# Graph network kernel: rebuilt eigenvector stage and changed Householder step

## The reference

```
deg = sum(A, axis=0) + sum(A, axis=1) - diagonal(A)
L_norm = d_inv_sqrt[:, None] * (diag(deg) - A) * d_inv_sqrt[None, :]
_, U = eigh(L_norm)
agg = einsum('mn,bnd->bmd', U.T, features)
h = relu(agg @ W1 + b1);  out = h @ W2 + b2
return einsum('nm,bmd->bnd', U, out)
```

## Time and profile before

| | us |
|---|---|
| median of 3 runs (lowest to highest) | 1511.3 (1510.47 to 1511.42) |
| profiled execution, its own time | 1511.8 |
| its span, first to last instruction | 1510.0 |

### The profile page before, as it was taken

The page is one execution under the profiler, slowest core; times in us unless marked ns, Lnnn a source line. Parts: engine busy times, 40 slices in busy tenths (PEclk is TensorE's granted clock), DMA queues, the critical chain, the costliest instruction groups (busy, mean ns, idle before and its releaser), DMA issues.

```text
span 1510.0 us, 22169 instructions
## 1 busy us (share of the span) xinstructions
PE 1105.1 (73%) x5407; PEld 673.1 (45%) x5407; DVE 1023.0 (68%) x4055; ACT 743.4 (49%) x2047; POOL 306.4 (20%) x1038
## 2 busy tenths in 40 slices
PE   3777777777542340158788568999999999479997
PEld 2444555555421130145453356444454444346665
DVE  7777887777779999855676744444434353757876
ACT  2444444444342436024466457775545554367775
POOL 4045555555346551000000000000011030000000
PEclk9999999999999995569998689999999999589999
DMA  5000000000110000000000000000000000000001
GB/s 143 1 1 1 1 1 1 1 2 1 22 31 1 1 0 1 1 0 0 0 0 0 0 0 0 0 0 0 1 0 0 0 1 0 0 8 21 28 21 36
DMA packets 16657, 12.33 MB, mean 8 GB/s; under 512 B 665, under 2 KB 14530, under 8 KB 16578
## 3 DMA queue, kind: packets, MB, share of 16 engines
q1 hardware_dynamic: 16578, 11.49, 2.7%
HBM read 7.23 MB, written 4.19 MB: 8 GB/s over the span
## 4 chain that ended last, share of the span: by engine, by line
PE 53%; DVE 32%; issue 6%; ACT 6%; DMA 1%; DVEq 1%; ACTq 0%; POOL 0%; POOLq 0%
PE P L1370 31%; PE P L704 10%; DVE scal L337 2%; ACT arena L656 2%; DVE arena L467 2%; PE P L1512 2%; DVE arena L521 2%; DVE arena L523 2%; DVE bst_all L922 1%; DVE arena L472 1%; DVE bcol L366 1%; ACT hb L1177 1%; DVE arena L465 1%; PE P L1505 1%; DVE arena L343 1%
## 5 line engine op out<-in xcount | busy, mean ns | idle before, releaser
L1370 PE MATMUL P<-arena,WT 128*128 (+2 forms) x792 | 329.0, 579 | 3.9 <-ACT L1263 2.9
L1370 PEld LDWEIGHTS P<-arena,WT 128*128 128x128 f32 x792 | 151.9, 192 | 181.0 <-issue 167.1
L704 PE MATMUL P<-arena 1*128 1x127 f32 (+62 forms) x504 | 163.0, 431 | 80.8 <-ACT arena L656 57.4
L1276 ACT ACTIVATE arena<-P,bl 128x512 f32<-128x512 f32 (+1 forms) x252 | 153.5, 636 | 139.0 <-PE P L1370 131.6
L704 PEld LDWEIGHTS P<-arena 1*128 1x128 f32 x504 | 124.1, 306 | 132.7 <-DVE arena L347 109.3
L911 POOL COPY arena<-arena 128x512 f32<-128x512 f32 x16 | 21.2, 1366 | 647.0 <-DVE arena L1101 555.2
L1090 DVE TENSOR_TENSOR arena<-arena 128x512 f32<-128x512 f32 (+1 forms) x36 | 22.0, 610 | 137.5 <-ACT arena L1276 137.5
L648 ACT ACTIVATE arena<-arena 1x127 f32<-1x127 f32 (+62 forms) x126 | 32.2, 256 | 154.9 <-DVE arena L358 144.6
L1177 ACT ACTIVATE hb<-xN,nmr,rsd 128x128 f32 (+1 forms) x192 | 78.6, 482 | 55.8 <-PE P L1370 46.9
L197 POOL TENSOR_SCALAR lf<-lf 1x1 f32<-1x1 f32 x210 | 86.1, 410 | 21.9
L704 PE MATMUL P<-arena,Ib 128*128 128x46 bf16 (+1 forms) x318 | 35.5, 273 | 64.0 <-ACT arena L678 63.4
(11 more groups left out here) (497 smaller groups left out, 2514.3 us busy)
## 6 DMA issues: line engine op xcount, KB each, us to landing
out_dram<-xN SPq DMA_DIRECT2D x16, 256.0 KB, 2.3
Wn<-in_L_gnn_Wih_dram SPq DMA_DIRECT2D x4, 256.0 KB, 2.9
Wn<-in_L_gnn_Whh_dram SPq DMA_DIRECT2D x4, 256.0 KB, 2.9
Wqkv<-in_L_gnn_W_dram SPq DMA_DIRECT2D x1, 192.0 KB, 3.6
W1n<-in_L_gnn_W_dram SPq DMA_DIRECT2D x1, 128.0 KB, 4.1
W2n<-in_L_gnn_W_dram SPq DMA_DIRECT2D x1, 128.0 KB, 3.9
Wg<-in_L_gnn_Wg_dram SPq DMA_DIRECT2D x2, 64.0 KB, 3.6
adj<-in_adj_dram SPq DMA_DIRECT2D x1, 64.0 KB, 1.8
```

The costliest lines, as they stand in the source:

```text
L704: def mm(o,l,r,start=True,stop=True): return t.matmul(o,lhsT=l,rhs=r,start=start,stop=stop)
L1276: act(s.gt[u][gate][:,0:cols],P[4*u+gate][:,0:cols],f,bias=s.bl[:,4*(p-1)+gate:4*(p-1)+gate+1]).then_inc(ev('lstm_gates'),1)
L1370: def mm(o,l,r,start=True,stop=True,**k): return t.matmul(o,lhsT=l,rhs=r,start=start,stop=stop,**k)
```

## The change

In the reflector loop:
- The floor operation on the norm goes; a constant of 1e-30 is given to the square root as its bias instead (a pointer). h is formed from the root alone.
- x becomes a column by a transpose instead of a product, and b becomes a row by a product over the columns k to 127 instead of a transpose over all 128.
- v is scaled as soon as the reciprocal is there: ScalarE does the elements from k+2 on, and VectorE the two in front, after the addition to x0 and behind Bv. The wait for the addition moves from p to this multiply.
- The first spot of leaf work moves from ahead of Bv to behind it.

In the eigenvector stage: three squares go to ScalarE and two products and the handling of the gaps go to GpSimd; the leaf sign is sent round in the recurrence; the seven signs come from one maximum, one comparison and one dot product in place of a chain; the eigenvalues of the first estimate are kept for both rounds of correction, so that gaps and their reciprocals are formed once, and Rayleigh quotients and the second and third row broadcast go; XnXn is multiplied earlier; input_variance, bias_columns and input_scale are put at other places.

Beside that, semaphores are merged (masks and iota; all parameters' loads; weights_T; residual_x and the like), with wait values to match. The diff, cut:

```diff
+        e=Chain(eng,ev('gpsimd_step'))
+        e.n=c.n
+        eng.wait_ge(ev('twisted'),1)
+        e.mark(tt(inv_up[:,1:N],inv_up[:,1:N],off[:,1:N],ALU.mult))
+        tt(inv_down[:,0:N-1],inv_down[:,0:N-1],off[:,1:N],ALU.mult).then_inc(ev('eigen_from_gpsimd'),1)
+        eng.wait_ge(ev('gaps'),1)
+        e(tt(far[:,:],gap[:,:],gap[:,:],ALU.mult))
+        e(ts(far[:,:],far[:,:],4e-12,None,ALU.is_ge))
+        e.mark(ts(half_near[:,:],far[:,:],0.5,-0.5,ALU.mult,ALU.add))
+        e(ts(near[:,:],far[:,:],-1.0,1.0,ALU.mult,ALU.add))
+        tt(gap[:,:],gap[:,:],near[:,:],ALU.add).then_inc(ev('eigen_from_gpsimd'),1)
         net.gpsimd_windows(eng)
...
-            c.mark(stt(scal[:,3:4],x0,-1.0,x0,ALU.mult,ALU.min))
-        sign_of_x0(0)
+            return c.mark(stt(scal[:,3:4],x0,-1.0,x0,ALU.mult,ALU.min))
+        signed=[sign_of_x0(0)]
         def hh_step(k):
             u,x_next=reflector(k),reflector(k+1)
             x0=u[:,k+1:k+2]
-            v.wait_ge(ev('column_norm2'),k+1)
-            floor=c.mark(ts(scal[:,4:5],scal[:,7:8],-1.0,-1e-30,ALU.mult,ALU.min))
-            c.wait(floor)
+            c.wait(signed[k])
             v.wait_ge(ev('column_norm'),k+1)
-            h=c.mark(ts(scal[:,2:3],scal[:,9:10],scal[:,3:4],scal[:,4:5],ALU.mult,ALU.add))
+            h=c.mark(stt(scal[:,2:3],scal[:,3:4],scal[:,9:10],scal[:,9:10],ALU.subtract,ALU.mult))
             sr=c.mark(ts(scal[:,1:2],scal[:,0:1],-1.0,scal[:,9:10],ALU.add,ALU.mult))
             c.wait(h)
-            ih=c.mark(v.reciprocal(scal[:,10:11],scal[:,2:3]))
-            c.wait(ih)
+            v.reciprocal(scal[:,10:11],scal[:,2:3]).then_inc(ev('v_scale'),1)
+            c.wait(sr)
             v.wait_ge(ev('column_psum'),k+1)
             tt(x0,x0,scal[:,1:2],ALU.add).then_inc(ev('v_unscaled'),1)
-            if k>=LEAF_FROM: leaf_at(2*(k-LEAF_FROM))
             v.wait_ge(ev('row_b'),k+1)
             v.wait_ge(ev('row_xB'),k+1)
             stt(Bv_row[:,k:N],b_row[:,k:N],scal[:,1:2],P[1][0:1,k:N],ALU.mult,ALU.add).then_inc(ev('Bv'),1)
+            v.wait_ge(ev('v_scale'),k+1)
             v.wait_ge(ev('v_unscaled'),k+1)
+            ts(v_row[:,k:k+2],u[:,k:k+2],scal[:,10:11],None,ALU.mult).then_inc(ev('v_scaled'),1)
+            if k>=LEAF_FROM: leaf_at(2*(k-LEAF_FROM))
             v.wait_ge(ev('Bv'),k+1)
             vp=c.mark(ttr(unused_row[:,k+1:N],u[:,k+1:N],Bv_row[:,k+1:N],scal[:,5:6]))
-            v.wait_ge(ev('v_scaled'),k+1)
+            v.wait_ge(ev('v_scaled'),2*k+2)
             x1=c.mark(stt(x1_row[:,k+2:N],Bv_row[:,k+2:N],v_row[:,k+1:k+2],b_row[:,k+2:N],ALU.mult,ALU.add))
...
+            if i==LEAF_SIGN:
+                v.wait_ge(ev('leaf_from_gpsimd'),5*SWEEPS-1)
+                tt(leaf[:,14:15],leaf[:,0:1],leaf[:,0:1],ALU.mult).then_inc(ev('leaf_sign'),1)
...
+        v.sem_inc(ev('twisted'),1)
         c(tt(G[:,:],G[:,:],D_down[:,:],ALU.subtract))
         c(tt(G[:,:],D_up[:,:],G[:,:],ALU.subtract))
-        c(tt(Y_work[:,:],D_down[:,:],D_down[:,:],ALU.mult))
-        c(tt(Y[:,:],D_up[:,:],D_up[:,:],ALU.mult))
+        c(tt(A_X[:,:],G[:,:],G[:,:],ALU.mult))
+        v.wait_ge(ev('squared'),2)
         c(tt(Y_work[:,:],Y_work[:,:],Y[:,:],ALU.add))
-        c(tt(Y[:,:],G[:,:],G[:,:],ALU.mult))
-        c(stt(Y_work[:,:],Y_work[:,:],(8*EPS)**2,Y[:,:],ALU.mult,ALU.add))
+        c(stt(Y_work[:,:],Y_work[:,:],(8*EPS)**2,A_X[:,:],ALU.mult,ALU.add))
...
-        c(ttr(Y_work[:,:],choice[:,:],G[:,:],col[:,6:7]))
-        c(ts(Y_work[:,:],choice[:,:],1.0,None,ALU.subtract))
-        c(tt(inv_up[:,1:N],inv_up[:,1:N],off[:,1:N],ALU.mult))
-        c(tt(inv_up[:,1:N],inv_up[:,1:N],Y_work[:,1:N],ALU.mult))
-        c(v.memset(inv_up[:,0:1],0.0))
-        c(tt(inv_down[:,0:N-1],inv_down[:,0:N-1],off[:,1:N],ALU.mult))
-        c(tt(inv_down[:,0:N-1],inv_down[:,0:N-1],Y_work[:,0:N-1],ALU.mult))
-        c(v.memset(inv_down[:,N-1:N],0.0))
-        c(v.tensor_tensor_scan(Y[:,:],inv_up[:,:],choice[:,:],0.0,ALU.mult,ALU.add))
+        c.mark(ttr(Y_work[:,:],choice[:,:],G[:,:],col[:,6:7]))
+        v.wait_ge(ev('eigen_from_gpsimd'),1)
+        up=c.mark(stt(inv_up[:,1:N],choice[:,1:N],-1.0,inv_up[:,1:N],ALU.add,ALU.mult))
+        down=c.mark(stt(inv_down[:,0:N-1],choice[:,0:N-1],-1.0,inv_down[:,0:N-1],ALU.add,ALU.mult))
+        c.wait(up)
+        c.mark(v.tensor_tensor_scan(Y[:,:],inv_up[:,:],choice[:,:],0.0,ALU.mult,ALU.add))
+        c.wait(down)
         c(v.tensor_tensor_scan(Y_work[:,::-1],inv_down[:,::-1],choice[:,::-1],0.0,ALU.mult,ALU.add))
...
+        ttr(Y_work[:,:],Y[:,:],Y[:,:],pair_state[:,2:3]).then_inc(ev('norm2'),1)
+        v.wait_ge(ev('norm2'),2)
         c(v.reciprocal(pair_state[:,3:4],pair_state[:,2:3]))
...
         v.wait_ge(ev('norm'),2)
-        c(v.reciprocal(pair_state[:,6:7],pair_state[:,1:2]))
-        c(ts(Y[:,:],Y[:,:],pair_state[:,6:7],None,ALU.mult))
...
+        norm=c.mark(v.reciprocal(pair_state[:,6:7],pair_state[:,1:2]))
+        ts(wide[:,0:N],I[:,:],pair_state[:,0:1],None,ALU.mult).then_inc(ev('eigenvalue_diagonal'),1)
+        c.wait(norm)
+        ts(Y[:,:],Y[:,:],pair_state[:,6:7],None,ALU.mult).then_inc(ev('Y_unit'),1)
+        eb,yb,ya=off[:,16::16],Y[:,16::16],Y[:,15:127:16]
+        c(ts(off_sign[:,:],eb,0.0,2.0,ALU.is_ge,ALU.mult))
+        v.wait_ge(ev('Y_unit'),1)
+        c(ts(block_mass[:,8:9],Y[:,0:1],0.0,2.0,ALU.is_ge,ALU.mult))
+        c(stt(bound_u[:,0:7],off_sign[:,:],-1.0,yb,ALU.add,ALU.mult))
         v.wait_ge(ev('leaf_sign_everywhere'),1)
...
+        c(ts(bound_u[:,7:8],block_mass[:,8:9],-1.0,P[4][:,0:1],ALU.add,ALU.mult))
+        c(tt(bound_u[:,0:7],bound_u[:,0:7],ya,ALU.add))
+        c(tt(bound_weight[:,0:7],bound_u[:,0:7],eb,ALU.mult))
...
+        c(stt(bound_weight[:,0:7],bound_weight[:,0:7],-1.0,bound_weight[:,0:7],ALU.mult,ALU.max))
+        c(ts(bound_u[:,0:7],bound_u[:,0:7],0.0,-2.0,ALU.is_ge,ALU.mult))
+        c(ts(bound_u[:,0:7],bound_u[:,0:7],1.0,None,ALU.add))
+        v.wait_ge(ev('squared'),3)
...
-        v.sem_inc(ev('eigenvalue_diagonal'),1)
+        c(stt(gate[:,:],gate[:,:],0.5,bound_order[:,:],ALU.is_gt,ALU.mult))
         v.wait_ge(ev('eigenvalue_row'),1)
         c(v.tensor_reduce(col[:,0:1],P[5][:,0:N],AX.X,ALU.max))
...
-        for b in (0,2,4,6,1,5,3):
-            c(ts(sign[:,1:2],bound_u[:,b:b+1],sign[:,0:1],None,ALU.subtract))
-            c(stt(sign[:,0:1],sign[:,1:2],bound_weight[:,b:b+1],sign[:,0:1],ALU.mult,ALU.add))
+        c(stt(bound_weight[:,0:7],bound_weight[:,0:7],col[:,0:1],gate[:,:],ALU.is_gt,ALU.mult))
+        c(v.tensor_reduce(col[:,1:2],bound_weight[:,:],AX.X,ALU.max))
+        c(ts(bound_weight[:,:],bound_weight[:,:],col[:,1:2],None,ALU.is_equal))
+        c(ttr(bound_weight[:,:],bound_weight[:,:],bound_u[:,:],sign[:,0:1]))
         ts(Y[:,:],Y[:,:],sign[:,0:1],None,ALU.mult).then_inc(ev('Y_ready'),1)
+        ts(gap[:,:],P[5][:,0:N],pair_state[:,0:1],None,ALU.subtract).then_inc(ev('gaps'),1)
+        net.input_variance(v)
         v.wait_ge(ev('Y_T_psum'),1)
         v.tensor_copy(Yt[:,:],P[0][:,0:N]).then_inc(ev('Y_T'),1)
-        net.input_variance(v)
+        net.bias_columns(v,c)
         v.wait_ge(ev('X_psum'),1)
         v.tensor_copy(X[:,:],P[2][:,0:N]).then_inc(ev('X_ready'),1)
-        net.bias_columns(v,c)
+        v.wait_ge(ev('X_ready'),1)
         for q in range(2):
             Xn,XTn=(X,XT) if q==0 else (U,UT)
-            v.wait_ge(ev('A_times_X'),q+1)
-            v.tensor_copy(A_X[:,:],P[3][:,0:N]).then_inc(ev('W_ready'),1)
+            c(tt(tmp[:,:],Xn[:,:],P[5][:,0:N],ALU.mult))
             if q==0:
+                v.wait_ge(ev('X_psum'),2)
                 c.mark(v.tensor_copy(XT[:,:],P[0][:,0:N]))
-                net.input_scale(v,c)
-            v.wait_ge(ev('S_and_G'),q+1)
...
-            c(ttr(tmp[:,:],Sx,I[:,:],col[:,0:1]))
-            c(ttr(tmp[:,:],Gx,I[:,:],col[:,1:2]))
-            c(v.reciprocal(col[:,2:3],col[:,1:2]))
-            c(ts(col[:,3:4],col[:,0:1],col[:,2:3],None,ALU.mult))
-            c(ts(wide[:,0:N],I[:,:],col[:,3:4],None,ALU.mult))
-            v.sem_inc(ev('eigenvalue_diagonal'),1)
...
-            v.wait_ge(ev('eigenvalue_row'),q+2)
...
-            c(v.reciprocal(Y_work[:,:],Y_work[:,:]))
...
-            v.sem_inc(ev('correction'),1)
+            v.wait_ge(ev('A_times_X'),2*q+1)
+            tt(A_X[:,:],P[3][:,0:N],tmp[:,:],ALU.subtract).then_inc(ev('W_ready'),1)
+            if q==0:
+                v.wait_ge(ev('eigen_from_gpsimd'),2)
+                c(v.reciprocal(inverse_gap[:,:],gap[:,:]))
+                c.mark(tt(inverse_gap[:,:],inverse_gap[:,:],far[:,:],ALU.mult))
+            v.wait_ge(ev('A_times_X'),2*q+2)
+            c(tt(G[:,:],P[2][:,0:N],half_near[:,:],ALU.mult))
+            half=c.mark(stt(G[:,:],I[:,:],0.5,G[:,:],ALU.mult,ALU.add))
+            v.wait_ge(ev('X_times_W'),q+1)
+            c(tt(tmp[:,:],P[1][:,0:N],inverse_gap[:,:],ALU.mult))
+            tt(G[:,:],tmp[:,:],G[:,:],ALU.add).then_inc(ev('correction'),1)
```

(30 more changed lines are left out.)

164 lines of the change are left out of this document (68 added, 96 removed).

## The result

The kernel after takes **1472.16 us** (median of 4 runs, 1470.52 to 1473.28) against 1511.16 (median of 4) of the kernel before: ratio 0.974, interval 0.9725 to 0.9759.

| stage, us | before | after | change | forecast |
|---|---|---|---|---|
| reflector loop | 379.15 | 361.69 | **-17.5** | -6.3 |
| its end to the twisted recurrence | 141.76 | 142.18 | +0.4 | 0 |
| twisted recurrence | 72.95 | 73.01 | +0.1 | +0.2 |
| eigenvector stage: to the unit Y | 8.37 | 6.55 | -1.8 | 7.4 |
| to the signed Y | 10.39 | 4.30 | -6.1 | 4.7 |

What follows compares the result with a forecast made beforehand. Chains of small dependent operations, not any engine's busy time, were taken as the bound. Profiled 1511.8 - 6.3 (loop) - 20.5 (eigenvector stage) + 0.2 (leaf sign) + 1.5 (GpSimd) = 1486.7, as median 1486 us; range 1478 to 1497.

Steps and rivals of the forecast that it cites:

- The ring over row_b, x*B, Bv, p, w: Reflector loop: the chain of dependent operations that sets the step time, 3.41 us in an early step; scalar chain not in it.
- the rival of the scalar chain: Reflector loop: the scalar chain is the bound, so 0.40 a step, 50 us, would go: 1442; chance 0.04.
- x column by transpose, -4.4: Reflector loop: one pass instead of two lets the column's copy start earlier; -4.4 us over 70 steps (0 to -8).
- Row of b by a product, +3.9: Reflector loop: two passes instead of one hold x*B longer in the first 55 steps; +3.9 us (+2.3 to +8.3).
- The two TensorE terms: Reflector loop: the row of b by a product, +3.9 us, and the x column by transpose, -4.4 us.
- Floor operation, 0: Reflector loop: removing the floor operation and one pointer of h gains 0, since both are off the ring.
- If that shrank by over 0.2: Reflector loop: condition on the zero for the floor; with over 0.2 less row_b/x*B work as cover, the norm would come late.
- The wait on Bv, -8.1: Reflector loop: p, with one wait instead of two, starts 0.065 us a step earlier; -8.1 us (-5 to -14, or 0).
- Leaf work behind Bv, +2.3: Reflector loop: leaf work moved from ahead of Bv to behind it makes p late in some 40 spots; +2.3 us (0 to +4).
- Eigenvector stage, -20.5 + 1.5: Eigenvector stage: 24.3 us against 44.8 by counting operations, -20.5, with 1.5 added for GpSimd.
- GpSimd's 1.5: Eigenvector stage: cost of GpSimd beside VectorE, 1.0 us for the first pair of products and 0.5 for the five gap operations.
- The slower rival (d): Reflector loop: the small multiply between Bv and p is fully exposed, 28 us over 125 steps: 1522; chance 0.05.

Runs made afterwards that it cites:

- xcol_product: Kernel after, with the x column again made by a product (two passes) instead of a transpose; 1484.88 us.
- column_after_root: Kernel after, with the x column's copy on ScalarE made to wait for the semaphore of the square root in front of it; 1483.82 us.
- root_no_bias: Kernel after, with the pointer bias taken off the square root, so no guard against a column of zeros; 1467.76 us.
- before_both: Kernel before, with the x column by a transpose and the row of b by a product, nothing else; 1508.39 us.
- p_two_waits: Kernel after, with p made to wait again for two semaphores, the x0 addition's ahead of Bv's; 1479.93 us.

## Why the prediction was wrong in size

- **What bounds the loop**: right for the kernel before. The ring over row_b, x*B, Bv, p, w is what every run moved, and the rival of the scalar chain as today's bound (1442) falls. That Bv "always" starts 0.10 after x*B isn't so: in 44 of the 124 steps leaf work stands in front of it, and these hold 9.2 of the 18.8 us of that gap.
- **x column by transpose, -4.4**: the step that failed. It let L652 start at the root's end, 0.28 after the root's start, where it starts at 0.20. In the kernel before the copy always found TensorE late (it starts 0.04 after the column's end on TensorE in every step), so its own rows could not show how it follows the root when neither waits: the two overlap by 0.09, the copy is 0.03 shorter, and the column is what starts x*B in nearly every step. xcol_product: 12.7. The same edit is worth 3.8 alone in the kernel before, so 4.4 was not far off for the edit by itself; it was wrong for the edit among the others. And the overlap could have been read ahead of the result, from other rows of the kernel before (reflector step of the earlier trace rows; counting stage):

```profile
42.54 0.30 ACT L648 ACTIVATE arena<-arena 1x121 f32<-1x121 f32 x1 [1.43 <-DVE arena L358]
42.75 0.18 ACT L648 ACTIVATION_READ_ACCUMULATOR arena<-arena 1x1 f32 x1
...
441.56 0.51 ACT L678 ACTIVATE arena<-arena 128x368 bf16<-128x368 f32 x1 [0.95 <-DVE arena L472]
441.97 0.46 ACT L666 ACTIVATE arena<-P 128x368 bf16<-128x368 f32 x1
```

The second of each pair starts some 0.09 before the first one's end (42.84; 442.07).

- **Row of b by a product, +3.9**: wrong in sign, -2.7 in the full change. The early cost is 2.8, inside its bounds. But the working stopped at step 55 with "and is cheaper after", and put no number on that: from step 38 on it is -5.5. And the product doesn't hold x*B's load for its two passes (0.44 to 0.51): the load goes in between, 0.20 after the row's at k=5. The two TensorE terms are off by 8.3 and 6.6 taken one at a time, and by 11.3 together, for they share slack.
- **Floor operation, 0**: wrong, by its own condition. "If that shrank by over 0.2" had to be set against the two TensorE terms above; the cover (from the next column of B to x*B's end) shrinks by 0.2 at k=97 and 0.3 at k=121, and with x*B so early the operation and the two-pointer h would have cost 7.8 (3.4 net of the shorter root).
- **The wait on Bv, -8.1**: 7.8. **Leaf work behind Bv, +2.3**: 4.1 (slightly over its bound of 4). From x*B's end to w the four gaps of VectorE changed by -5.8 in the traces, forecast -5.8; since the two runs give -3.7, that match is partly luck (2.6 of it lies between p and w, where nothing was forecast).
- **Eigenvector stage, -20.5 + 1.5**: -21.1. The counts held to 0.4 us a part; GpSimd's 1.5 was too much, the first pair costs 0.38, and the five operations for the gaps no idle time that the trace shows.
- **The slower rival (d)**: the small multiply delays p by nothing (0.06 after Bv). It has another effect: the first outer product now waits for it, and in the last 25 steps the way from w to the next column of B is 1.4 us longer in sum, which fits that wait, though no run tested it. It was not priced.
- **Open**: which share of the growth of the column's worth, from some 4 to 12.7, is the shorter scalar chain's and which the leaf work's, for no run has the one without the other in the kernel before. The stretch from the loop's end to the recurrence takes 140.9 to 141.5 us in ten of the sixteen traces and 141.8 to 142.4 in six, those of before and after among them; no run was made for it. Nor was the network's -1.1 followed up: the full clock comes back 3.0 us after its first product instead of 5.1.

The chances given (0.60 to the forecast, 0.04 to a much larger gain) were too narrow on the fast side. The terms were bounded one by one, and each bound kept the others' present values; but these edits free one another, and their joint effect lies outside the root of the sum of squares.

## To carry to other kernels

Where a ring of short operations has a second and a third chain close behind it, price the edits as a set: after each term, recompute which input of the joining instruction comes last. The column's transpose gave 3.8 alone, some 4 on top of the row's product, and 12.7 in the full change, where the scalar chain is shorter and the leaf work out of Bv's way. Put filler work in front of an instruction that waits for another engine, not behind it, as long as that wait is there: with both TensorE edits in the kernel before, a leaf step lost 0.15 us in front of Bv and another step 0.08. And a formula that is cheaper at one size and dearer at another needs a number on both sides of the crossing, which may then be used as a switch.

## What the runs showed of the hardware

- Two ScalarE instructions that don't wait for one another overlap by 0.09 us in the records (247.02 against 247.11, and the pairs of the kernel before above); in column_after_root a wait between them costs that, some 0.03 more before the start and 0.03 of duration (0.17 instead of 0.14).
- The root with a pointer as bias takes 293 ns in the kernel after, without one 202 in root_no_bias.
- Behind a transpose on TensorE the next load waits for 0.30 us; behind a product of the same operand form it goes when its input is there, but not before 0.19 at 123 columns and 0.10 at 31 (before_both), and the two products' passes overlap, each then longer (0.62 instead of 0.57 for x*B).
- A second, long fulfilled semaphore in front of a VectorE instruction delays it by 0.085 us (p 0.144 after Bv's end instead of 0.059, p_two_waits).
